# Cross-attention: order of maxima, low halves and the context cast on VectorE, and the place of two waits on TensorE

## The reference

```python
def _L0_xattn_ref(queries, context, wq, bq, wk, bk, wv, bv, wo, bo):
    q = queries @ wq.T + bq
    k = context @ wk.T + bk
    v = context @ wv.T + bv
    # 16 heads of 32
    attn = jnp.einsum('bhnd,bhsd->bhns', q, k) * scale
    attn = jax.nn.softmax(attn, axis=-1)
    out = jnp.einsum('bhns,bhsd->bhnd', attn, v)
    return out.transpose(0, 2, 1, 3).reshape(B, NQ, D) @ wo.T + bo

x = x + _L0_xattn_ref(_layernorm(x), ctx_1024, ...)   # x: (16, 128, 512), ctx_1024: (16, 2048, 512)
```

## Time and profile before

| what | us |
|---|---|
| median of 3 runs | 3999.93 (3994.23 to 4001.72) |
| profiled execution | 3999.69 |
| its span | 3997.6 |
| PE busy in the span | 3833.1 (96%) |
| VectorE busy | 2815.2 (70%) |
| ScalarE busy | 1751.8 (44%) |
| GpSimd busy | 1285.3 (32%) |
| mean granted TensorE clock | 0.991 of full speed |

### The profile page before, as it was taken

How to read it: one execution, slowest core, us unless ns; L and a number is a source line. 1 busy time by engine, 2 the same in 40 slices (tenths; PEclk the granted TensorE clock), 3 DMA queues, 4 the chain that set the end, 5 groups by cost and what they waited for, 6 DMA issues and landing times.

```text
span 3997.6 us, 83589 instructions
## 1 busy us (share of the span) xinstructions
PE 3833.1 (96%) x34880; PEld 2809.5 (70%) x34880; DVE 2815.2 (70%) x2964; ACT 1751.8 (44%) x3490; POOL 1285.3 (32%) x604
## 2 busy tenths in 40 slices
PE   8999999999999999999999998999999998799998
PEld 6777777777877777777777776555455554388886
DVE  5667667667657667667666756999999999855443
ACT  2324324424414423423433435777777778422221
POOL 1111111111011011011111112888888888821011
PEclk9999999999999999999999998999999999999999
DMA  4110110110110011010011023112211122120000
GB/s 155 38 43 29 39 43 29 39 43 29 38 53 31 29 51 31 29 51 31 29 51 40 33 67 101 33 37 64 59 59 34 42 64 85 37 77 22 32 23 21
DMA packets 96902, 183.73 MB, mean 46 GB/s; under 512 B 8450, under 2 KB 12930, under 8 KB 96547
## 3 DMA queue, kind: packets, MB, share of 16 engines
q1 hardware_dynamic: 96546, 178.27, 13.9%
HBM read 152.82 MB, written 25.43 MB: 45 GB/s over the span
## 4 chain that ended last, share of the span: by engine, by line
PE 78%; DVE 10%; POOL 5%; ACT 3%; issue 3%; DMA 0%; DVEq 0%; POOLq 0%; ACTq 0%; SPq 0%
PE scores L523 31%; PE scores L602 8%; PE o_acc L616 6%; PE b_y L1444 6%; PE c_acc L1961 4%; PE c_ring L1946 4%; DVE max_parts L407 4%; DVE b_decay L1299 3%; PE scores L596 3%; POOL b_drive L1009 2%; PE b_work L1356 2%; PE scores L571 2%; PE b_work L1405 2%; PE c_experts_ps L1993 1%; PE b_work L1341 1%
## 5 line engine op out<-in xcount | busy, mean ns | idle before, releaser
L244 POOL TENSOR_TENSOR c_lo<-c_raw,c_hi 128x2048 fp32r<-128x2048 f32 x64 | 294.9, 4607 | 1974.5 <-DVE c_hi L346 1974.5
L434 DVE TENSOR_TENSOR prob_sums<-prob_sums,probs 128x1024 f32<-128x1024 f32 x480 | 566.7, 1222 | 115.3 <-ACT probs L319 115.3
L1009 POOL TENSOR_TENSOR b_drive<-b_dt_u,b_bc 128x1024 f32<-128x1024 f32 x256 | 600.0, 2357 | 112.8 <-PE b_y L1444 79.0
L407 DVE TENSOR_REDUCE max_parts<-scores 128x2 f32<-128x1024 f32 x512 | 602.0, 1218 | 40.6 <-PE scores L571 40.6
L319 ACT ACTIVATE probs<-scores 128x512 f32<-128x512 f32 x1024 | 528.9, 604 | 215.3 <-PE scores L602 213.8
L399 DVE SCALAR_TENSOR_TENSOR k_lo<-scores,bk_sb,k_hi 128x512 fp32r<-128x512 f32 x256 | 192.3, 751 | 565.5 <-ACT k_hi L304 565.5
L1444 PE MATMUL b_y<-b_drive,b_ident 128*128 128x512 f32 x1024 | 497.0, 615 | 73.2 <-DVE b_drive L1310 51.9
L1299 DVE TENSOR_TENSOR_SCAN b_decay<-b_decay,b_drive 128x1024 f32<-128x1024 f32 x217 | 496.5, 2288 | 12.9 <-ACT b_decay L1167 9.2
L304 ACT ACTIVATE k_hi<-scores,bk_sb 128x512 fp32r<-128x512 f32 x256 | 176.3, 689 | 604.7 <-PE scores L523 604.7
L312 ACT COPY v_sb<-scores 128x512 f32<-128x512 f32 x240 | 140.8, 587 | 669.1 <-PE scores L523 669.1
L1167 ACT ACTIVATE b_decay<-b_dt,b_a 128x254 f32<-128x254 f32 x1024 | 425.1, 461 | 0.4
(11 more groups left out here) (231 smaller groups left out, 6506.3 us busy)
## 6 DMA issues: line engine op xcount, KB each, us to landing
c_raw<-in_ctx SPq DMA_DIRECT2D x64, 1024.0 KB, 5.2
b_bc<-bc_scratch SPq DMA_DIRECT2D x128, 256.0 KB, 4.3
c_w_raw<-in_mlp_w SPq DMA_DIRECT2D x16, 512.0 KB, 3.6
q_scratch<-v_sb SPq DMA_DIRECT2D x4, 1024.0 KB, 4.3
q_raw<-q_scratch SPq DMA_DIRECT2D x16, 256.0 KB, 5.1
q_raw<-in_x SPq DMA_DIRECT2D x16, 256.0 KB, 2.7
x_scratch<-q_raw SPq DMA_DIRECT2D x16, 256.0 KB, 5.8
attn_scratch<-attn_out_sb SPq DMA_DIRECT2D x16, 256.0 KB, 2.0
```

The lines of the kernel that those rows point to most:

```text
L244: pool.tensor_tensor(c_lo[:, slot], c_raw[:], c_hi[:, slot].bitcast(F32), ALU.subtract).then_inc(c_lo_ready, 1)
L407: dve.tensor_reduce(max_parts[:, g, 2 * pair:2 * pair + 2, s], max_banks[:, 2 * pair:2 * pair + 2, :], AX.X, ALU.max).then_inc(max_taken, 1)
L434: dve.tensor_tensor(part, part, probs[:, u % 4], ALU.add).then_inc(summed, 1)
L1009: pool.tensor_tensor(drive[:, m % 4], dt_u[:, 2 * p:2 * p + 2, :].unsqueeze(1).to_broadcast([P, SG, 2, T]), bc[:, g, 0].unsqueeze(2).to_br ...
```

## The change

VectorE, in each block: the maxima of group g now come ahead of the low half of group g + 2. The cast of the next context block (high_part) no longer stands ahead of maxima 2; it stands at the head of the block, ahead of low half 0, and in a batch's first block between low half 0 and low half 1. Its condition is the same: products of block n - 1 ended (proj_ready) and data there (ctx_loaded).

PE: score_for_max had two waits ahead of M0 of a batch, for the split queries (q_split) and for all exponentials of the batch before (exp_done). They now stand in enter, ahead of K2.

Nothing else is changed; the instructions that compute are the same in number and shape.

```diff
@@ run_vector, batch
                     n = i * blocks + s
+                    more = s < blocks - 1 or not last
+                    if s > 0 and more:
+                        dve.wait_ge(proj_ready, n * 2 * chunks)
+                        high_part(n + 1, (s + 1) % 2)
                     low_keys(n, s, 0)
+                    if s == 0:
+                        if not first:
+                            dve.wait_ge(proj_ready, n * 2 * chunks)
+                        high_part(n + 1, (s + 1) % 2)
                     low_keys(n, s, 1)
                     if s == 0 and not first:
                         divide(i - 1, 0)
                     for g in range(chunks):
+                        reduce_max(i, s, g)
                         if g + 2 < chunks:
                             low_keys(n, s, g + 2)
-                        if g == 2 and (s < blocks - 1 or not last):
-                            if s > 0 or not first:
-                                dve.wait_ge(proj_ready, n * 2 * chunks)
-                            high_part(n + 1, (s + 1) % 2)
-                        reduce_max(i, s, g)
@@ run_tensor
-            def score_for_max(i, s, g, first):
-
-                if s == 0 and g == 0:
-                    pe.wait_ge(q_split, i * 2 + 2)
-                    if not first:
-                        pe.wait_ge(exp_done, i * exp_units)
+            def score_for_max(i, s, g):
+
                 pe.wait_ge(k_hi_ready, (i * blocks + s) * chunks + g + 1)
@@ run_tensor, enter
                 if not first:
                     sum_over_keys(i - 1)
+                pe.wait_ge(q_split, i * 2 + 2)
+                if not first:
+                    pe.wait_ge(exp_done, i * exp_units)
                 project_k(i, 0, 2, first)
```

## The result

The changed kernel takes 3970.07 us (median of 6 runs, 3968.16 to 3972.77); the kernel before takes 3998.14 (6 runs, the three shown above among them). The ratio is 0.9932, 95% interval 0.9921 to 0.9942: 28 us less, where 32 was forecast. The profiled execution took 3968.16 with a span of 3966.1, 31.5 us less than the span before. The medians differ by less than the two spans, since the profiled execution of before (3999.69) lies above the median of its runs and this one is the fastest of its own.

The account below looks back on a forecast made before the run. PE was taken to bound the kernel, its score groups waiting for VectorE's maxima. -34.5 + 3.3 - 1.0 = -32.2 us took 3999.7 to 3967.5 us, range 3960 to 3976, or 3958 to 3983 to hold 8 in 10.

Parts of the forecast that it names:

- What bounds the kernel: Attention stage: PE sets the end; its score groups wait for VectorE's maxima, 27.7 us in 66 waits.
- The maxima first, the cast out of the middle: Attention blocks: first to fourth score group falls from 10.71 to 10.17 us in the loop; 34.5 us saved with written-out blocks.
- free distance: PE's time from one score group to the next when nothing holds it: 3.39 us, read from the last block.
- the seven blocks written out: First and last batch without the very first block: 0.62 us gained each, 4.3 us together.
- The cast at its new place: Head of each block, in VectorE's idle time before the first low half: the 1.22 us cast costs nothing.
- The first block: Very first attention block: the cast waits for data not yet landed, 3.3 us lost once, bounds 0 and 7.7.
- The query waits: Start of each batch on PE: moving two waits gains 1 us, bounds 3.1 gained and 0.3 lost.
- VectorE beside GpSimd: Low halves beside c_lo: not held; two-SBUF-input contention, about 0.5 us in each of 15 batches, left out of the sum.
- (a): Rival: c_lo holds each block's first low half, 88 us lost against 32 gained, 4056 us; chance 5%.
- (b): Rival: low halves delay the value projections, giving back 13 to 25 us, 3980 to 3993 us; chance 13%.
- (c): Rival: no change, PE gives the saved wait back later in the block, 4002 us; chance 6%.
- The slower case: Outcome for the whole kernel: slower than before, because c_lo holds the low half; chance 0.05.

Follow-up runs that it names:

- the two kernels with operations added: Changed kernel plus unused 256-column VectorE operations beside GpSimd's c_lo: additions and a copy in one, scans and additions in the other; 3972.66 and 3970.1 us.
- the short maxima: Changed kernel with the maxima taken over only the first 128 of each 512 scores; one execution, 3970.68 us.
- the three traces with the early load: Changed kernel with context block 1's load issued ahead of the last query store (twice) or right behind it: 3964.42, 3966.02 and 3967.07 us.

## Why the prediction was right, and where it was off

**What bounds the kernel** was right: PE, with one wait in each of 64 blocks. The row is gone, and the time went with it. Of the loop's 0.48 per block, 0.44 was this wait ahead of M1; that M3 came just as the maxima let it, as the prediction read, cost nothing yet, since it was not late behind M2 (3.40).

**The maxima first, the cast out of the middle**: right, by its own steps. The places of R0, L2, R1 and M1 came within 0.05 of those worked out, V0 and V1 start 0.43 to 0.44 behind M1 and M2, as where nothing holds them, although only some 0.2 is left to them. The term was 3 us too large, because the free distance was taken as 3.39 three times from one block; it is 3.41 to 3.42 in two of three in the loop. The prediction's range had that. For the seven blocks written out it took 10.79 from the very first block, which is not one of the seven; their mean was 10.80, so that this term fitted is in part luck.

**The cast at its new place** costs nothing outside the first block, as worked out: 2.12 us of idle time are left behind it, 1.05 in the second block of a batch, and L1 of a batch's first block still has 2.07 ahead of it. And alone it gains nothing; the prediction did not say so in so many words, but its steps (M1 waits for R0 behind L2) do.

**The first block** was mis-sized: 4.8 (4.5 to 5.4 in four other traces with this order) in place of 3.3. The landing at 82.9, the cast and L1 came to 0.1 us as forecast, K3 to 0.2. What failed is the step from K3's start to M1, 2.95, taken from a row in which PE had not stood still: after 3.8 us of standing it took 4.54 us at a granted clock of 0.63. One could have known to ask: the stall was itself part of the forecast.

**The query waits**: right in kind, too small in size, 1.0 in place of 2.7 in this trace; with the waits alone it was 1.3. The third that it took was a guess, and the sum wanders too much between executions to be priced well.

**VectorE beside GpSimd**: the reading was wrong. The prediction took the scans and products of the state-space stage for operations with two SBUF inputs, without looking up where their tiles lie; b_decay is in PSUM, so the two busy shares say nothing against the rule. The division's step was held in all 15 batches. It cost nothing, because it was held only until c_lo's end, not also behind GpSimd's addition that follows (the prediction's price by the rule was 7.5 us), and R0 was due 0.9 later anyway. That the sum could leave it out was luck: the reason given for it was false. The part of it on which the sum hung, that low halves (PSUM and one SBUF input) run freely beside c_lo, was right: 0.74 to 0.75 in all 256.

**The rivals**: (a) fell with that. (b) fell, V0 and V1 start at their free distance. (c) fell. The slower case never came near.

The measured 3970.1 lies 2.6 above the forecast of 3967.5 and within the narrower of its ranges, 3960 to 3976. By the spans the change gained 29.4 us in place of 32.2, and the two errors of 3 and 1.5 us one way and the one of 1.7 the other account for that. By the medians it gained 28.1; the forecast was counted from 3999.7, 1.6 above the median of all six runs of the kernel before, which hid part of the difference.

## What to carry to other kernels

When an engine that is waited for has two kinds of work in a row, put what releases the bound engine first and what it needs later second, and move what nobody needs soon into a gap; then work both orders through from one start, to see whether two moves need each other, as here. Before moving a step ahead of others, look at the first pass through it, where its data may not be there yet: here that one block ate 5 of some 34 us, and a small edit, of VectorE's order or of SP's, gave them back. A stall of the matrix engine must be priced together with the clock behind it. And before busy shares are set against a rule on memories, look up in which memory each operand lies.

## What the runs showed of the hardware

- After standing still for 3.4 to 3.8 us in the first block, TensorE had a granted clock of 0.50 to 0.63 over the next 4.6 us (six traces: the changed kernel and its repetition, the cast alone, the two kernels with operations added, the short maxima); after 2.2 us in the same place it kept 1.00 (one trace).
- A VectorE addition or scan with two SBUF inputs, and a copy within SBUF, each of 256 columns, took 2.0 to 3.5 us beside a GpSimd subtraction and ended 0.15 to 0.56 after it; without it beside them the addition took 0.41 and the copy 0.28. Operations with one input from PSUM and one from SBUF did not notice it (0.74 to 0.75 for 512 columns).
- A 1 MB load issued 0.4 us behind a 1 MB store landed 7.4 to 7.6 us after its issue, where 5.2 is the median of such loads, and the store landed after 5.1 to 5.3 in place of 4.3 (the three traces with the early load).
